# Four graph layers on one core: edge codes kept as pairs of bf16, six source tables by ScalarE, the third layer's input in six parts, and another order of the first loads

## The reference, cut to what matters

```python
h = relu(layernorm(x)); x += segment_sum(edge_weight[:, None] * h[dst], src) @ W + bias
h = relu(layernorm(x)); x += (1 + eps) * h + segment_sum(relu(h[src] + edge_attr), dst)
h = relu(layernorm(x)); x += (D^-1/2 (A + I) D^-1/2)^2 h         # sums over r = src of rows c = dst
h = relu(layernorm(x)); x += the same matrix, degrees of src, transposed and applied once
```

## Time and profile before

| what | us |
|---|---|
| time, median of 3 runs | 10917.36 (10911.26 to 10933.73) |
| the profiled execution, its own time | 10818.04 |
| its span, first to last instruction | 10816.2 |
| PE, PEld, DVE, ACT, POOL busy in the span | 6417.2, 5569.8, 4776.5, 3992.4, 4088.1 |
| share of the chain that ended last: PE, unknown queue, issue, DVE, ACT | 38%, 25%, 13%, 8%, 8% |

### The profile page before, as it was taken

The page is one execution under the profiler, slowest core; times in us unless marked ns, Lnnn a source line. Parts: engine busy times, 40 slices in busy tenths (PEclk is TensorE's granted clock), DMA queues, the critical chain, the costliest instruction groups (busy, mean ns, idle before and its releaser), DMA issues.

```text
span 10816.2 us, 266700 instructions
## 1 busy us (share of the span) xinstructions
PE 6417.2 (59%) x100278; PEld 5569.8 (51%) x100279; DVE 4776.5 (44%) x7168; ACT 3992.4 (37%) x6938; POOL 4088.1 (38%) x4193
## 2 busy tenths in 40 slices
PE   5444444444444444444444444445999979999999
PEld 4333333333333333333333333335888879999998
DVE  5444444444444444444444443448999940111000
ACT  3333333333333333333333333335888820000333
POOL 2444444444444444444444444443888820000000
PEclk6666666666666666666666666667999989999999
DMA  6444444444444444444444444445999978888998
GB/s 172 141 146 146 143 143 140 142 138 146 144 144 146 147 144 142 139 137 142 145 146 147 147 142 138 145 148 180 317 317 317 316 247 265 275 279 273 195 204 178
DMA packets 1738803, 1964.50 MB, mean 182 GB/s; under 512 B 897469, under 2 KB 1403119, under 8 KB 1737791
## 3 DMA queue, kind: packets, MB, share of 16 engines
q1 hardware_dynamic: 1337520, 1347.06, 43.2%
q10 hardware_dynamic: 300646, 448.79, 12.1%
q0 software_dynamic: 100000, 158.60, 4.7%
HBM read 1258.29 MB, written 618.65 MB: 174 GB/s over the span
## 4 chain that ended last, share of the span: by engine, by line
PE 38%; another core or an unknown queue 25%; issue 13%; DVE 8%; ACT 8%; ACTq 3%; DMA 2%; POOL 1%; SPq 1%; DVEq 1%; POOLq 0%
PE pG L2174 7%; PE pT L2057 6%; ACT stg L2431 4%; PE pG L2013 3%; PE pT L2061 2%; PE pT L2174 2%; PE pG L2024 2%; PE pG L2226 2%; PE pR L2174 2%; PE pG L2022 2%; PE pG L2213 2%; DVE msum L1825 2%; ACT dfar L2398 1%; PE pG L2138 1%
## 5 line engine op out<-in xcount | busy, mean ns | idle before, releaser
L1359 POOL DMA_INDIRECT recB<-rec,qpos x3125 | 3046.9, 975 | 4294.4 <-issue 3403.0
L2057 PE MATMUL pT<-soh,doh 128*128 128x128 bf16 x10600 | 1771.6, 268 | 3412.7 <-ACT stg L2431 3032.7
L2431 ACT CAST stg<-pT 128x512 fp8e4<-128x512 f32 x2650 | 1499.7, 585 | 3989.4 <-remote 3050.9
L2057 PEld LDWEIGHTS pT<-soh,doh 128*128 128x128 bf16 x10600 | 1027.9, 117 | 3642.7 <-ACT stg L2431 3154.7
L1641 DVE TENSOR_TENSOR rec<-pG,wN 128x480 f32<-128x480 f32 x314 | 205.5, 654 | 2252.6 <-PE pG L2013 2241.9
L1628 DVE TENSOR_TENSOR soh<-smd,pG 128x1280 bf16<-128x1280 bf16 x530 | 432.5, 816 | 1314.4 <-remote 866.9
L2061 PE MATMUL pT<-car,qidb 128*128 128x256 fp8e4 x2597 | 925.1, 356 | 0.0
L2138 PE MATMUL pG<-mpl,doh 128*128 128x144 bf16 x10388 | 764.3, 227 | 34.0 <-POOL mpl L1380 25.0
L1628 DVE TENSOR_TENSOR doh<-dm,pG 128x2560 bf16<-128x2560 bf16 x530 | 782.7, 1477 | 1.5 <-ACT dm L2509 0.9
L1628 DVE TENSOR_TENSOR doh<-smd,pG 128x2560 bf16<-128x2560 bf16 x530 | 783.1, 1478 | 0.0
L2138 PEld LDWEIGHTS pG<-mpl,doh 128*128 128x128 bf16 x10388 | 666.0, 96 | 63.6 <-POOL mpl L1380 49.1
(11 more groups left out here) (266 smaller groups left out, 14329.2 us busy)
## 6 DMA issues: line engine op xcount, KB each, us to landing
recB<-zt ACTq DMA_DIRECT2D x102, 2425.5 KB
brec<-recB SPq DMA_DIRECT2D x477, 495.0 KB
erec<-recB SPq DMA_DIRECT2D x477, 495.0 KB, 5.5
cl<-cA SPq DMA_DIRECT2D x80, 2560.0 KB, 10.8
cA<-stg ACTq DMA_DIRECT2D x530, 320.0 KB
cl<-cA SPq DMA_DIRECT2D x40, 2720.0 KB, 11.1
drow<-dlD SPq DMA_DIRECT2D x157, 640.0 KB, 5.8
srowB<-srD SPq DMA_DIRECT2D x265, 320.0 KB, 5.8
```

Of the source, the lines that this page charges most:

```text
L1359: p.indirect_dma_start(recF, bass.IndirectOffsetOnAxis(ap=qpos[:, s, c:c + 1], axis=0), rec[:, s, c, :], None).then_inc(s_sc[s], 16)
L2057: ins = t.matmul(bank[:, h * 256 + b * 128:h * 256 + b * 128 + 128], doh[:, o, 2 * e + b, h * 128:(h + 1) * 128], soh[:, o, 2 * e + b, :], ...
L2431: a.copy(stg[:, o, :, e * 256:(e + 1) * 256], B8[6 + (g * 5 + e) % 2][:, :].rearrange("p (h x) -> p h x", h=2), saturate=False).then_inc(e ...
```

## The change

1. *Codes as pairs.* In columns 97 and 98 of a record each 4-byte place holds the code twice as bf16 in place of once as f32 (`rec_u`, `brec_u`, `erec_u`, `zt_u` are the bf16 views). `one_hots` reads the pair where it lies in the record; `places`, `smd`, `codes`, `dm5` and their semaphores are gone; the copy to `smK` reads the record.
2. *Six sources by ACT.* `sT` is built by ACT for groups 1, 3, 4, 6, 8, 9 and by DVE for 0, 2, 5, 7. `srowB` of the six comes from `srD8`.
3. *The layer in six parts.* `part` is loaded, normed and multiplied in the six units `UN`. The buffer `cl0` and the parts 0 and 1 have places and loads of their own inside the last three chunks of layer 1. All loads of `part` are SP's.
4. *Front.* The zeros of chunk 0 go out on SP right after the memset of `zt`, with a semaphore of their own; the zeros of chunk 1 and the rest of x go out after h W is loaded again for the first slots.
5. One more check value in `chk` (its column 9), since the early parts of `part` must be complete by chunk 49.

```diff
-        smd = pha("smd", [128, 5, GB, 2, 2], BF16)
...
-        dm5 = phb("dm5", [128, 5, GB, 2], BF16)
...
+        cl1 = phc("cl1", [128, 18, GB * 64], BF16)
+        cl2 = phc("cl2", [128, 18, GB * 64], BF16)
...
+        phd = Placer(nc, max(phb.off, phc.off))
+        ct = Placer(nc, phd.off)("ct", [128, 6, 8 * 128], BF16)
+        pl0 = Placer(nc, phd.off + 6 * 8 * 128 * 2)("pl0", [128, 8, GB * 64], BF16)
+        cl0 = phd("cl0", [128, 18, GB * 64], BF16)
...
+        UP = [(k0, k0 + nk) for k0, nk in UN]
...
+        KL = 49
...
+        BY_ACT = [1, 3, 4, 6, 8, 9]
+        BY_DVE = [g for g in range(JG) if g not in BY_ACT]
+
         def rowed(K, g):
 
-            return (m_sU, K * 5 + (g + 1) // 2) if g % 2 else (m_sT, K * 5 + g // 2 + 1)
+            return (m_sU, K * len(BY_ACT) + BY_ACT.index(g) + 1) if g in BY_ACT else \
+                (m_sT, K * len(BY_DVE) + BY_DVE.index(g) + 1)
...
-                    p.wait_ge(q_ld[2], 64)
+                    p.wait_ge(s_p0, 32)
...
-                v.wait_ge(e_sm, c + 1)
+                v.wait_ge(l_b[r], K * 64 + (g // 5 * 32 + 32))
                 reached(v, e_ca, c * 5 - 5)
-                one_hots(soh[:, o, :, :], smd[:, r, :, 0, :], GB, 128, ioA)
-                v.wait_ge(l_b[r], K * 64 + (g // 5 * 32 + 32))
+                one_hots(soh[:, o, :, :], brec_u[:, r, :, 97, :], GB, 128, ioA)
...
-                one_hots(doh[:, o, :, :], smd[:, r, :, 1, :], GB, 256, ioA)
+                one_hots(doh[:, o, :, :], brec_u[:, r, :, 98, :], GB, 256, ioA)
...
-                    if g % 2 == 0:
+                    if g in BY_DVE:
...
-                    v.wait_ge(m_dm, c + 1)
+                    v.wait_ge(k_e[r], K * 32 + (g // 5 * 16 + 16))
                     reached(v, m_sc, c - 4)
-                    one_hots(doh5[:, r, :, :], dm5[:, r, :, :], GB, 256, ioB).then_inc(m_do, 1)
+                    one_hots(doh5[:, r, :, :], erec_u[:, r, :, 98, :], GB, 256, ioB).then_inc(m_do, 1)
...
-                collect(NK - 1, (NK - 1) % 2)
-                nch.mark("free")
-                for b, (lo, hi) in enumerate(HALF):
-                    v.wait_ge(s_half[b], 32)
+
+                def centred(u):
+
+                    lo, hi = UP[u]
+                    v.wait_ge(s_half[u % 2], u // 2 * 32 + 32)
                     nch(v.tensor_tensor(qx3[:, lo:hi, :], qx3[:, lo:hi, :], qh3[:, lo:hi, :], ALU.add))
                     nch(v.tensor_tensor(qx3[:, lo:hi, :], qx3[:, lo:hi, :], scr[:, lo:hi, :], ALU.add))
-                    centre(2, b, qx3, qst)
-                summed(2, SQ2, hs_)
-                for b in range(2):
-                    scaled(2, b, SQ2, True)
-                    rests(2, b, xpc, qh3, qh_u, scr, scr_u)
+                    nch(v.tensor_reduce(qst[:, 0, lo:hi], qx3[:, lo:hi, :], AX.X, ALU.add))
+                    nch(v.tensor_scalar(qst[:, 1, lo:hi], qst[:, 0, lo:hi], 1.0 / D, None, ALU.mult))
+                    nch(v.tensor_tensor(qh3[:, lo:hi, :], qx3[:, lo:hi, :], bc(qst[:, 1, lo:hi], D), ALU.subtract))
+                    nch.mark(f"cen2{u}")
+
+                def varied(u):
+
+                    lo, hi = UP[u]
+                    v.wait_ge(t_sq, sqn[f"sq{u}"])
+                    nch(v.tensor_reduce(qst[:, 2, lo:hi], scr[:, lo:hi, :], AX.X, ALU.add))
+                    nch.mark(f"var2{u}")
+
+                def normed(u):
+
+                    lo, hi = UP[u]
+                    v.wait_ge(t_sq, sqn[f"rt{u}"])
+                    nch(v.reciprocal(qst[:, 4, lo:hi], qst[:, 3, lo:hi]))
+                    nch(v.tensor_tensor(qst[:, 4, lo:hi], qst[:, 4, lo:hi], qdi[:, lo:hi], ALU.mult))
+                    nch(v.scalar_tensor_tensor(out=qh3[:, lo:hi, :], in0=qh3[:, lo:hi, :], scalar=0.0,
+                                               in1=bc(qst[:, 4, lo:hi], D), op0=ALU.max, op1=ALU.mult))
+                    nch.mark(f"nrm2{u}")
+                    nch(v.tensor_tensor(scr[:, lo:hi, :], qh3[:, lo:hi, :], qh_u[:, lo:hi, :], ALU.subtract))
+                    nch.mark(f"res2{u}")
+                    nch(v.tensor_tensor(xpc[:, lo:hi, 2, :], scr[:, lo:hi, :], scr_u[:, lo:hi, :], ALU.subtract))
+                    nch.mark(f"pcs2{u}")
...
+                centred(0)
+                collect(NK - 1, (NK - 1) % 2)
+                varied(0)
+                normed(0)
+                centred(1)
+                varied(1)
+                normed(1)
+                centred(2)
+                for u in range(2, len(UN)):
+                    varied(u)
+                    if u + 1 < len(UN):
+                        centred(u + 1)
+                    normed(u)
...
+                t.wait_ge(m_ev, NK)
...
+                                t.wait_ge(e_qn, qn[f"pcs2{u}"])
+                                t.wait_ge(t_sq, sqn[f"lo{u}"])
...
-            def places(K, g):
-                c = K * JG + g
-                r = g % 5
-                a.wait_ge(l_b[r], K * 64 + (g // 5 * 32 + 32))
-                reached(a, e_pl, c - 4)
-                a.copy(smd[:, r, :, :, :],
-                       brec[:, r, :, 97:99].unsqueeze(3).to_broadcast([128, GB, 2, 2])).then_inc(e_sm, 1)
-
             def bucket(K, g, known):
                 c = K * JG + g
                 o = g % 2
-                if g == JG - 1:
-                    if not (known and K == NK - 1):
-                        places(K + 1, 0)
-                elif g == 0:
-                    places(K, 1)
-                    places(K, 2)
-                elif g < JG - 2:
-                    places(K, g + 2)
-                a.copy(smK[:, g * GB:(g + 1) * GB], smd[:, g % 5, :, 0, 0])
+                a.wait_ge(l_b[g % 5], K * 64 + (g // 5 * 32 + 32))
+                a.copy(smK[:, g * GB:(g + 1) * GB], brec_u[:, g % 5, :, 97, 1])
...
-                def codes(K, g):
-                    c = K * JG + g
-                    r = g % 5
-                    a.wait_ge(k_e[r], K * 32 + (g // 5 * 16 + 16))
-                    reached(a, m_do, c - 4)
-                    a.copy(dm5[:, r, :, :], erec[:, r, :, 98:99].to_broadcast([128, GB, 2])).then_inc(m_dm, 1)
...
-                    if not (known and K == NK - 1 and g >= JG - 2):
-                        codes(K + (g + 2) // JG, (g + 2) % JG)
...
-                    n = g + (2 if o else 3)
-                    if not (known and K == NK - 1 and n >= JG):
-                        (none_away if o else distances)(K + n // JG, n % JG)
-
-                codes(0, 0)
-                codes(0, 1)
+                    for n, part_ in ((g + 2, none_away), (g + 3, distances)):
+                        if n % JG in BY_ACT and not (known and K == NK - 1 and n >= JG):
+                            part_(K + n // JG, n % JG)
...
-            sp.dma_start(qx3[:, 8:NB - 1, :], x[8 * 128:(NB - 1) * 128, :].rearrange("(j p) d -> p j d", p=128)
-                         ).then_inc(q_ld[3], 16)
             sp.wait_ge(e_q, qm["c0"])
-            sp.dma_start(qx3[0:N - (NB - 1) * 128, NB - 1, :], x[(NB - 1) * 128:N, :]).then_inc(q_ld[3], 16)
             sp.dma_start(hT[NP:NPX, :].rearrange("(p r) c -> p (r c)", p=128),
                          zz[:, 0:144].bitcast(BF16)).then_inc(q_st, 16)
             sp.wait_ge(e_q, qm["zt"])
+            for h in range(2):
+                prefill(sp, 0, h, s_p0)
...
+                held(sp, e_cv, (c - 5) * 5 + 1)
...
-            sp.wait_ge(q_ld[2], 32)
-            for h in range(2):
-                prefill(sp, 0, h, q_ld[2])
             sp.wait_ge(e_q, qm["codes"])
             load_ea(0, 2)
+            sp.wait_ge(q_ld[0], 48)
             for h in range(2):
                 prefill(sp, 1, h)
-            sp.wait_ge(q_ld[0], 48)
+            sp.dma_start(qx3[:, 8:NB - 1, :], x[8 * 128:(NB - 1) * 128, :].rearrange("(j p) d -> p j d", p=128)
+                         ).then_inc(q_ld[3], 16)
+            sp.dma_start(qx3[0:N - (NB - 1) * 128, NB - 1, :], x[(NB - 1) * 128:N, :]).then_inc(q_ld[3], 16)
...
-                    held(sp, m_dm, c - 4)
...
+                    tab, w = (srD8, 64) if g in BY_ACT else (srD, 128)
...
+                def load_part(u):
+
+                    lo, hi = UP[u]
+                    if u >= 2:
+                        hold(sp, s_half[u % 2], u // 2 * 32)
+                    sp.dma_start(qh3[:, lo:hi, :], part[lo * 128:hi * 128, :].rearrange("(j p) c -> p j c", p=128)
+                                 ).then_inc(s_half[u % 2], 16)
+                    sp.dma_start(scr[:, lo:hi, :], part[NPX + lo * 128:NPX + hi * 128, :].rearrange("(j p) c -> p j c", p=128)
+                                 ).then_inc(s_half[u % 2], 16)
+
+                for g in range(JG):
+                    step(0, g, True)
+                with sp.Fori(1, NK - 3) as K:
+                    for g in range(JG):
+                        step(K, g, False)
+                for K in range(NK - 3, NK):
+                    for g in range(JG):
+                        step(K, g, K == NK - 1)
```

(42 more changed lines are left out.)

92 lines of the change are left out of this document (55 added, 37 removed).

## The result

The changed kernel takes 11393.26 us (median of 4 runs, 11371.83 to 11411.24) where the one before takes 10920.31 in the same comparison: a ratio of 1.0431, 95% interval 1.0409 to 1.0453. I had forecast 10810; it is 473 us slower than before, not 107 faster.

The account below looks back on a forecast made before the run. Latencies and waits were taken to bound the sorting stage, DVE layer 1 (DMA close behind), and PE the dense layers. Gains of 26 + 34 + 38 + 9 = 107 us off the median 10917.36 gave 10810 us, range 10735 to 10895.

Parts of the forecast that it names:

- codes as pairs: Sorting stage: ACT loses 530 copies of codes, 26 us gained (nothing to 69); in layer 1 worth nothing by itself.
- rival C: Layer 1's one-hots: codes read inside records drop them to one element per cycle, 726 us lost, 11536; chance 0.04.
- Rival D: Sorting stage: another order of waits can be worse, 0.9 us in each of 157 slots, 141 us, 10977; chance 0.07.
- the distance from first to last scatter: Sorting stage, sign of being wrong: this distance, 78.8 to 7342.6 us before, has grown.
- ACT as a releaser for over 15 us in layer 1: Layer 1, sign of being wrong: DVE or PE wait for ACT more than 15 us.
- the hidden waits of the earlier trace: Sorting stage: semaphore waits with senders not shown, 38.5% of its chain, might leave the copies' removal worth nothing.
- Six sources: Layer 1: ACT builds six sT in ten, DVE four; 34 us gained (26 to 38.7), a chunk 22.9 us.
- DVE's sT count: Layer 1, sign of being right: DVE builds sT 212 times in place of 265.
- this lumpiness: Layer 1: adjacent ACT-built groups make ACT's relu up to 1 us late; charged 0.1 us a chunk.
- Six parts: Last message to first dense product: PE starts 49.2 us earlier, idle 5 to 7 us; net 38 us (33 to 46).
- The early loads: Layer 1's last 2.6 chunks: 15.5 us of added DMA work make DVE stand 11 us (3 to 16).
- The front: Start of kernel: first scatter at 67 us in place of 78.79; 9 us gained (0 to 12).

Follow-up runs that it names:

- a_pad60: The changed kernel with 60 already satisfied waits at the start of ScalarE's program: 10755.47 us, 0.9958 of the kernel before.
- b_pad25: Control: the kernel before with 25 already satisfied waits at the start of ScalarE's program: 10816.5 us, 1.0005 of the kernel before.
- a_places: Changed kernel, loop inside the window, sorting stage's code copies two groups ahead as before, without SyncE's added wait: 10756.96 us, 0.9963 of the kernel before.
- a_pad60c: The same kernel as a_pad60, on a further chip beside a_places: 10735.85 us, 0.9940 of the kernel before.
- a_late60: a_pad60 with the early loads issued after layer 1's last message instead of inside its last three chunks: 10956.23 us, kernel before 10901.77.

## Why the prediction was wrong

**The step that failed is the first, codes as pairs.** It priced the copy's time on ACT (0.13 us each, 26 us) and held that, apart from slower one-hots (rival C), no row spoke of a loss. What decided was that 20 instructions fewer in the loop and 11 fewer ahead of it put the loop's start across a block boundary of ACT's code. Where the loop lies among the fetched blocks was no term of the sum, and it outweighed every term that was. Price: the difference between 1.0431 and 1.0046 or 1.0042, some 420 us (on different chips); 8.8 us for each of 49 passes of ACT's loop in the profiles, 430 us. A pass has two holes of 7.2 and 5.2 us where there was one of 1.9. Rival D had the right stage and sign, but as waits in another order, 0.9 us in each of 157 slots; it was a fetch, once a chunk, in every third slot. Of the signs of being wrong, the distance from first to last scatter did grow. ACT as a releaser for over 15 us in layer 1 came true as well (53.5 us in 1000), but the kernel before has 38.1 there, so this sign could tell nothing.

**The rest of part 1** is not one number. With the loop in place the sorting stage takes 7249 us (a_pad60) where the old order (b_pad25) takes 7279 on the same chip, one profiled execution each, that of b_pad25 21 us above its median. On another chip a_places, with the copies where they were, is 21 us slower than a_pad60c in the medians. So 10 to 30 us were won there. That this is the size of my 26 is partly luck: the sum took 0.13 us for a copy, and one put back directly ahead of the casts costs 84 and 87 us in all, 0.16 us each over all 530, where I counted four groups in ten. On two other chips it takes 7442 to 7465, some 200 more, while the whole of the old kernel is only about 95 us longer there: some 100 us lost. That it is part 1 which does this is not shown, since a_places was not run on those two; the cause of this loss of about 0.4% stays open. I had named the hidden waits of the earlier trace rows as what could swallow the gain; that it could turn by chip I had not seen.

**Six sources** had the right direction and the wrong size: 11 us measured for 34. DVE's sT count is 212, as said, but DVE no longer ends every step. Waits of DVE, PE and ACT in 1000 us of layer 1 of the changed kernel (us in total, times, longest):

```profile
DVE msum L1846 <- PE pG L2182: 16.9, 43, 0.5
...
PE pG L2182 <- ACT sT L2559: 53.5, 85, 0.9
...
ACT mpl L2567 <- PE pG L2194: 101.7, 170, 1.1
```

Once a chunk (43 times in 42.7 chunks) DVE waits 0.4 us for PE, which waits for ACT's sT. I had charged this lumpiness 0.1 us a chunk; a chunk is 23.42 us between branches in the median, 23.65 before, 22.9 forecast.

**Six parts** came out as worked: 12.8 us from last message to first product (11.1 said), PE idle 6.51 us (5 to 7), one later pause of 1.9. The difference is in the short operations, which are longer than the 0.97 scaled from the earlier trace rows at first. DVE in order of time:

```profile
9340.74 0.66 DVE L1846 TENSOR_TENSOR msum<-pG,erec 128x480 f32<-128x480 f32 x1 [1.87 <-PE pG L2182]
9341.32 1.45 DVE L1857 TENSOR_TENSOR qx<-qx,qa 128x816 f32<-128x816 f32 x1
9342.81 1.68 DVE L1858 TENSOR_TENSOR qx<-qx,scr 128x816 f32<-128x816 f32 x1
...
9346.46 1.01 DVE L1861 TENSOR_TENSOR qa<-qx,qst 128x816 f32<-128x816 f32 x1
```

The early loads cost 12.6 us of layer 1 by a_late60 (11 said); that they buy just as much later, so that they were worth nothing, I had not put in the sum as a choice.

**The front** was right: the first scatter at 69.2 (67 said), the second slot at 85.20 where it was 94.28, 9 us earlier. Against the earlier trace rows:

```profile
46.58 1.31 ACTq L2391 DMA_DIRECT2D hw<-hT  x2
49.39 1.36 ACT L2456 ACTIVATE dfar<-drow,pcs 128x1280 bf16<-128x1280 bf16 x1 [2.89 <-DMA drow<-dlD]
...
69.21 1.11 POOL L1380 DMA_INDIRECT recB<-rec,qpos  x1 [66.97 <-ACT rec L2447]
...
85.20 0.96 POOL L1380 DMA_INDIRECT recB<-rec,qpos  x1 [9.81 <-issue]
```

**The one-hots** read the pair inside a record at full speed, so rival C did not happen, and the rule of the Trainium skill ("VectorE: DVE Perf Modes", section "Mode 2×_1P — pack two bf16 into one 32-bit read") holds for this layout too. Groups of the page:

```profile
L1650 DVE TENSOR_TENSOR doh<-erec,pG 128x2560 bf16<-128x2560 bf16 x530 | 782.3, 1476 | 15.3 <-DMA erec<-recB 15.3
L1650 DVE TENSOR_TENSOR soh<-brec,pG 128x1280 bf16<-128x1280 bf16 x530 | 432.7, 816 | 1353.9 <-PE pT L2113 1056.1
```

## What to carry to other kernels

Before pricing an edit inside a loop, count the instructions between its branches on each engine, and read the profile's instruction queues: where a loop nearly fills what is held, removing instructions can cost more than they did. An idle "issue" of microseconds directly behind a loop's branch, with several packets in the instruction queue for each pass, was a code fetch here, and a few dozen waits that are already satisfied, put ahead of the loop, test it. Compare a change of a latency-bound stage on more than one chip: 0.994 and 1.004 are the same kernel here.

## What the runs showed of the hardware

Code for ScalarE came in packets of 8192 bytes, and loops stayed free of fetches only where they lay within three such blocks counted from the one of their first instruction (eight kernels). Each pass of one that didn't took about five packets and a stop of 5.2 to 5.3 us behind the branch, and a further one at the next block's first instruction: 5.2 us where that lay 9 instructions behind the head, 2.1 at 17, 0.8 at 26, none at 39. The kernel before took 10788 to 10920 us (medians) in five comparisons and 7638 on one chip, where ScalarE's casts proceed during POOL's bursts (mostly 15 to 20 in each, elsewhere 4 to 9). A VectorE sum of 816 f32 elements took 1.45 and 1.68 us where later ones of the same size took 1.01; at the same time two of GpSimd's additions of 480 elements took 1.63 and 1.75 us, which take 0.99 otherwise.
